# Four one-hot comparisons of 512 columns become one of 2048, and the index rows in DRAM become four times as long

## The reference

```python
x = x + attention(x, cond)                   # 16 heads, modulated by cond
x = x + sample(x, grid=cond)                 # linear interpolation along the channels
x = x + gru(cond, x)                         # 64 steps
x = x + oscillators_rk4(cond, cond, x)       # 64 steps
```

```python
ix = (grid + 1.0) * 0.5 * (L - 1)            # L = 512, clipped to the row
i0 = floor(ix)
out = (1 - w1) * x[..., i0] + w1 * x[..., i0 + 1]
```

## Time and profile before

| what | value |
| --- | --- |
| median of the runs | 1525.3 us (1524.68 to 1526.01) |
| profiled execution | 1528.0 us, span of its instructions 1526.2 us |
| TensorE busy | 1472.8 us, 97% of the span |
| VectorE busy | 1322.9 us, 87% |
| ScalarE, GpSimd busy | 902.6 us (59%), 756.9 us (50%) |
| L776, the builds | 256 instructions, 145.9 us busy |
| DMA, slices 2 to 16 of 40 | busy tenths 2 to 7, 52 to 130 GB/s |
| load of an index row | 64 of 128 KB, 3.0 us from issue to landing |
| store of an output row (L1976) | 63 of 128 KB, 1.7 us |

### The profile page before, as it was taken

One profiled execution on the slowest core, in us unless ns is written; L12 is line 12 of the kernel. 1 busy time (PEld: TensorE's weight loads), 2 busy tenths in 40 slices (PEclk: granted clock), 3 DMA queues, 4 the chain that ended last, 5 costly groups with the idle time before them and its releaser, 6 DMA issues.

```text
span 1526.2 us, 95000 instructions
## 1 busy us (share of the span) xinstructions
PE 1472.8 (97%) x42214; PEld 1308.4 (86%) x42214; DVE 1322.9 (87%) x3190; ACT 902.6 (59%) x2753; POOL 756.9 (50%) x916
## 2 busy tenths in 40 slices
PE   4799999999999999999999999999999999999997
PEld 2466677666776668999999999999999999999996
DVE  5888989988889878688888888888888888888887
ACT  5566776667766653555555555555555555555553
POOL 2567666666666754534434443443444344344432
PEclk9999999999999999999999999999999999999999
DMA  7255444545455432000000000000000000000000
GB/s 255 52 114 115 108 106 104 116 118 120 127 118 130 96 102 87 8 15 12 15 15 15 12 16 15 12 15 15 15 12 15 15 12 15 15 15 12 15 15 14
DMA packets 122602, 84.03 MB, mean 55 GB/s; under 512 B 68656, under 2 KB 107824, under 8 KB 122192
## 3 DMA queue, kind: packets, MB, share of 16 engines
q1 hardware_dynamic: 121968, 77.87, 20.3%
q10 hardware_dynamic: 224, 0.09, 0.0%
HBM read 42.23 MB, written 11.60 MB: 35 GB/s over the span
## 4 chain that ended last, share of the span: by engine, by line
PE 91%; DVE 4%; issue 2%; POOL 1%; ACT 1%; DMA 1%; SPq 0%; DVEq 0%; ACTq 0%; POOLq 0%
PE psB L1432 34%; PE psA L1461 15%; PE psQ L1146 15%; PE psA L1466 8%; PE psQ L1188 7%; PE psO L1234 5%; PE psO L1222 2%; PE psB L1170 2%; PE psA L1124 2%; DMA front<-in_cond 1%; POOL S L434 0%; DVE psO L1645 0%; POOL front L453 0%; DVE room L880 0%; PE psQ L1202 0%
## 5 line engine op out<-in xcount | busy, mean ns | idle before, releaser
L1432 PE MATMUL psB<-first,Wx 128*128 128x64 f16 x9216 | 290.3, 193 | 1.4 <-issue 1.1
L1432 PE MATMUL psB<-first,Whh 128*128 128x64 f16 x9072 | 287.0, 193 | 1.3 <-POOL first L1897 0.5
L1461 PE MATMUL psA<-ts,Cp 128*128 128x64 f16 x8160 | 280.7, 193 | 6.0 <-ACT ts L1532 6.0
L1432 PEld LDWEIGHTS psB<-first,Wx 128*128 128x128 f16 x9216 | 277.9, 98 | 2.0 <-issue 1.7
L1432 PEld LDWEIGHTS psB<-first,Whh 128*128 128x128 f16 x9072 | 274.1, 98 | 2.3 <-issue 1.4
L1146 PE MATMUL psQ<-Wx,front 128*128 128x512 f16 x1152 | 269.0, 384 | 4.1 <-DVE front L952 4.0
L1461 PEld LDWEIGHTS psA<-ts,Cp 128*128 128x128 f16 x8160 | 256.2, 98 | 7.0 <-ACT ts L1532 6.8
L1532 ACT ACTIVATE ts<-qst 128x256 f16<-128x256 f32 x192 | 80.1, 417 | 297.9 <-DVE qst L1645 297.9
L1146 PEld LDWEIGHTS psQ<-Wx,front 128*128 128x128 f16 x1152 | 108.9, 99 | 124.5 <-issue 5.0
L1897 POOL TENSOR_TENSOR en<-rz,dn 128x256 f32<-128x256 f32 x64 | 46.7, 730 | 259.8 <-issue 257.1
L1466 PE MATMUL psA<-ts,Cp 128*128 128x64 f16 x4080 | 161.2, 193 | 0.3 <-issue 0.3
(11 more groups left out here) (194 smaller groups left out, 2890.4 us busy)
## 6 DMA issues: line engine op xcount, KB each, us to landing
front<-in_x SPq DMA_DIRECT2D x32, 256.0 KB, 3.1
XR<-in_x_turned SPq DMA_DIRECT2D x32, 256.0 KB, 3.4
rows<-rows_dram SPq DMA_DIRECT2D x64, 128.0 KB, 3.0
out<-ob SPq DMA_DIRECT2D x63, 128.0 KB, 1.7
x<-x SPq DMA_DIRECT2D x29, 224.0 KB
Whh<-in_W_qkv SPq DMA_DIRECT2D x12, 256.0 KB, 8.4
room<-in_W_hh SPq DMA_DIRECT2D x12, 256.0 KB, 2.7
room<-in_W_ih SPq DMA_DIRECT2D x12, 256.0 KB, 3.0
```

The lines of the kernel that those rows point to most:

```text
L1432: last = mm(o, W_[:, i, c, g * PART:(g + 1) * PART], src[:, j, c, :], start=False, stop=False, skip_group_check=True)
L1461: mm(psF[:, s % 2, m, :], Cp[:, i, c, m * PART:(m + 1) * PART], ts_[:, 0, c, :], start=(c == 0 and m == 0 and i == 0), stop=False, skip_gr ...
```

## The change

`rows_dram` gets four versions of each index row: version c holds i0 - 128 c, so that each is to be compared with p alone. `lidx` shrinks to one column, `rows` grows from 512 to 2048 elements per partition, and `build` becomes one instruction over 2048 elements. It can't be split over two places of a slot any more, so it stands whole in one of them. `grid_rows` writes the four versions with four instructions in place of one cast. The kernel also asks for a smaller scratch area for descriptors (`dynamic_dma_scratch_size=2048`), which makes room for the longer rows.

```diff
-    lidx, gqk = sb("lidx", [PART, KC]), sb("gqk", [PART, 1])
+    lidx, gqk = sb("lidx", [PART, 1]), sb("gqk", [PART, 1])
-    rows = [sb(f"rows{u}", [PART, D], F16) for u in range(2)]
+    rows = [sb(f"rows{u}", [PART, KC, D], F16) for u in range(2)]
...
         def load_rows(p, b):
             need(sp, e_built, p.n * 2 + b - 1)
-            sp.dma_start(rows[b][:, :], rows_dram[bass.ds(p.n * 2 + b, 1), :].rearrange("a n -> (a n)")
-                         .partition_broadcast(PART)).then_inc(rows_in[b], 16)
+            sp.dma_start(rows[b][:, :, :].rearrange("p c n -> p (c n)"), rows_dram[bass.ds(p.n * 2 + b, 1), :, :]
+                         .rearrange("a c n -> (a c n)").partition_broadcast(PART)).then_inc(rows_in[b], 16)
...
-        def build(p, b, chunks):
-            if chunks[0] == 0:
-                dve.wait_ge(rows_in[b], p.n * 16 + 16)
...
-            for k in chunks:
-                e = v.tensor_scalar(E_of(p, b)[:, k, :], rows[b][:, :], lidx[:, k:k + 1], None, ALU.is_equal)
-            if chunks[-1] == KC - 1:
-                e.then_inc(e_built, 1)
+        def build(p, b):
+            dve.wait_ge(rows_in[b], p.n * 16 + 16)
...
+            v.tensor_scalar(E_of(p, b).rearrange("p c n -> p (c n)"), rows[b][:, :, :].rearrange("p c n -> p (c n)"),
+                            lidx[:, 0:1], None, ALU.is_equal).then_inc(e_built, 1)
...
-            v.tensor_copy(i0h, i0).then_inc(rows_ready, 1)
+            for c in range(KC):
+                last = v.tensor_scalar(i0h[:, c, :], i0, 1.0, float(-c * PART), ALU.mult, ALU.add)
+            last.then_inc(rows_ready, 1)
```

More of the change, by code:

```diff
@@ L179, in attention_and_sampling @@
     iint = w1.bitcast(I32)
-    i0h = rows[0][0:B, :]
+    i0h = rows[0][0:B, :, :]
     psA, psB, psQ, psO = (banks[n] for n in ("psA", "psB", "psQ", "psO"))
@@ L340, in slot @@
                 sp.wait_ge(rows_ready, 1)
-                sp.dma_start(rows_dram, i0h).then_inc(rows_out, 16)
+                sp.dma_start(rows_dram.rearrange("b c n -> b (c n)"), i0h.rearrange("b c n -> b (c n)")).then_inc(rows_out, 16)
                 sp.wait_ge(rows_out, 16)
@@ L387, in _ @@
                                 pattern=[[-1, PART]], channel_multiplier=1).then_inc(consts, 1)
-        nc.gpsimd.iota(lidx[:, :], pattern=[[PART, KC]], base=0, channel_multiplier=1,
+        nc.gpsimd.iota(lidx[:, :], pattern=[[0, 1]], base=0, channel_multiplier=1,
                        allow_small_or_imprecise_dtypes=True).then_inc(consts, 1)
@@ L761, in scale_x @@
                             rsT.unsqueeze(1).broadcast_to([PART, KC, PART]), ALU.mult).then_inc(xr_done, 1)
-        def build(p, b, chunks):
-            if chunks[0] == 0:
-                dve.wait_ge(rows_in[b], p.n * 16 + 16)
[L766 to L774, removed]
-            for k in chunks:
-                e = v.tensor_scalar(E_of(p, b)[:, k, :], rows[b][:, :], lidx[:, k:k + 1], None, ALU.is_equal)
-            if chunks[-1] == KC - 1:
-                e.then_inc(e_built, 1)
+        def build(p, b):
+            dve.wait_ge(rows_in[b], p.n * 16 + 16)
+            if p.n < NP - 1:
+                need(dve, samp_done, p.n * 2 + b - 1)
+            elif b == 1:
+                for u in range(2):
+                    dve.wait_ge(wih_out[u], 3 * KC // 2 * 16)
+            if p.n == 0:
+                dve.wait_ge(consts, 3)
+                dve.wait_ge(cp_lo, KC)
+                dve.wait_ge(wo_lo, KC)
+            v.tensor_scalar(E_of(p, b).rearrange("p c n -> p (c n)"), rows[b][:, :, :].rearrange("p c n -> p (c n)"),
+                            lidx[:, 0:1], None, ALU.is_equal).then_inc(e_built, 1)
         def means(cols, qk, x):
@@ L976, in slot @@
                 grid_middle()
-            if tap and tap.n > 0:
-                build(tap, 0, (0,))
             if p := pair(-1):
@@ L982, in slot @@
             if tap:
-                build(tap, 0, (1, 2, 3) if tap.n > 0 else range(KC))
+                build(tap, 0)
             if i == 1:
@@ L1002, in slot @@
                 grid_weight()
-            if tap:
-                build(tap, 1, (0, 1))
             if p := pair(-2):
@@ L1013, in slot @@
             if tap:
-                build(tap, 1, (2, 3))
+                build(tap, 1)
             if p := pair(-1):
@@ L1060, in _ @@
             slot(*pairs_at(i))
-        build(N3, 0, (0,))
         low_qk(N1, 0)
         low_qk(N1, 1)
-        build(N3, 0, (1, 2, 3))
+        build(N3, 0)
         sums_qk(N0, 0)
         least(N1)
-        build(N3, 1, (0, 1, 2))
         sums_qk(N0, 1)
@@ L1072, in _ @@
         scale_qk(N0)
-        build(N3, 1, (3,))
+        build(N3, 1)
         low_o(N2)
@@ L1092, in _ @@
         weigh_taps(N3, 1)
-        build(N2, 0, range(KC))
+        build(N2, 0)
         low_p(N0, 0)
         low_p(N0, 1)
-        build(N2, 1, (0,))
+        build(N2, 1)
         residual(N1)
-        build(N2, 1, (1, 2, 3))
         weigh_taps(N2, 0)
         low_o(N0)
-        build(N1, 0, range(KC))
+        build(N1, 0)
         weigh_taps(N2, 1)
-        build(N1, 1, range(KC))
+        build(N1, 1)
         residual(N0)
         weigh_taps(N1, 0)
-        build(N0, 0, range(KC))
+        build(N0, 0)
         weigh_taps(N1, 1)
-        build(N0, 1, range(KC))
+        build(N0, 1)
         dve.wait_ge(S_["th_done"], 1)
@@ L1986 @@
     from concourse.bass_utils import run_bass_kernel_spmd
-    nc = bacc.Bacc("TRN2", target_bir_lowering=False, num_devices=1)
+    nc = bacc.Bacc("TRN2", target_bir_lowering=False, num_devices=1, dynamic_dma_scratch_size=2048)
     x, cond = inputs["x"], inputs["cond_2048"]
@@ L2007 @@
     out = nc.dram_tensor("out", (T, PART, KC * B), F32, kind="ExternalOutput").ap()
-    rows = nc.dram_tensor("rows_dram", (B, D), F16, kind="Internal").ap()
+    rows = nc.dram_tensor("rows_dram", (B, KC, D), F16, kind="Internal").ap()
     wih = nc.dram_tensor("wih_dram", (D, 2, 3 * D), F16, kind="Internal").ap()
```

## The result

The changed kernel took 1528.45 us in the median of 20 executions, against 1526.67 us of the kernel before in 20 on the same chip. The two medians differ by 1.8 us; the ratio worked out from all the executions is 1.0022, with a 95% interval from 1.0012 to 1.0032: slower by some 3.4 us. Timed once more on another chip, it was 1.0033 [1.0021, 1.0045], and the kernel before against itself 0.9996 [0.9985, 1.0006]. The mean of the two ratios of the change is 1.0027, or 4.2 us of 1526. The median lies within the predicted range, and the ratio just past the 0.2% that the prediction took as no change, on the slower side. (In the excerpt of the order of the changed kernel's steady slot, the query/key subtractions stand with L748 and L751; in the profile they are L751 and L754.)

A forecast was written before the change was run, and what follows sets the result against it. TensorE, busy for 97% of the span, was taken to bound the kernel. The terms +3.0 - 0.3 + 0 + 0 gave +2.7 us, and against the median of 1525.3 a forecast of 1528.0 us, range 1524.8 to 1532.

The forecast's parts named there:

- The build: VectorE's one-hot build: one takes 0.7 to 1.8 us where four cost 1.2 to 3.0; booked at 0 in steady slots.
- The piece ahead of the subtraction: Slot at 95 us: removing a build piece before the query/key subtraction ends TensorE's 0.34 us wait, -0.3 us once.
- The index rows: Start, slot 2: four operations replace one cast on VectorE, taking turns with GpSimd; +3.0 us, handed on whole to TensorE.
- the upper: Upper bound for the index rows at the start: all three added copies take a full turn with GpSimd, +3.5 us.
- The wait for oT: Start of the kernel: the delayed copies lengthen TensorE's wait for oT from 1.18 to 4.2 us.
- The clock: TensorE's 1.2 GHz stretch, 78.36 to 81.70 us: taken as 0, with -1.7 and +1.5 us kept open.
- the rival that the loss vanishes: TensorE's low-clock loss at the start disappears, -1.7 us, giving 1526.3 us; chance 2.5 in 10.
- The loads: Row loads growing from 128 to 512 KB land at 3 to 3.5 us and cost 0 us in the slots.
- the slow rival: Row loads keep 85 GB/s, delaying x1 in the slots and the end: 1530 to 1558 us; chance 1.5 in 10.
- The tail: After the last slot: +0.2 us on the projection behind low_o(N2), -0.2 at the last build; together 0, from -0.2 to +0.5.
- the relief of TensorE: Steady slots: VectorE's saved 0.3 us reaches TensorE 26 times, worth 7.8 us, giving 1520.5; chance 0.4 in 10.
- the copies that slip through: Start: the added index copies run at their lone pace of 0.42 us each; +0.1 us, 1525.4; chance 1 in 10.

The follow-up runs named there:

- the copies alone: The kernel before with three more index-copy operations behind its cast, into spare buffers, nothing else of the change; ratio 1.0016, repeated 1.0011.
- the two with the loads twice: The changed kernel with every row load issued again into a spare buffer, 1.0094; the same with single loads in the last three pairs, 1.0055.
- the kernel with the loads alone: The kernel before with 512 KB row loads, its one cast row stored four times, comparisons reading the first quarter; ratio 1.0010, repeated 1.0022.

## Why the prediction was right, step by step

The forecast was 1528.0 and the median 1528.45, inside the range. But two terms were wrong, in opposite directions, and their errors nearly cancel: that the number came out so close is luck. It is luck, too, that 1528.45 is so near to 1528.0; the kernel before took 1526.67 in the same series, not the 1525.3 that the forecast started from. The mechanism of the copies is there, but smaller than forecast; that of the loads' cost the prediction doesn't have.

**The build, 0.7 to 1.8 us, no gain in the steady slots: right.** 0.70 to 1.46, median 0.74. The cover was TensorE's own work: VectorE's time for the builds went from 145.9 to 57.6 us, and in the same stretch its idle time grew (ahead of the sums of squares, L795, 48.8 us in 100 to 560, for ScalarE; 17.5 before). Putting the four comparisons back changed nothing either. A slot without a pause stayed at 17.25 us.

**The piece ahead of the subtraction, -0.3 us: the wait right, the gain not seen.** The wait of 0.34 at 96.63 is gone at 95.53, but the scores come 18.18 us after the last ones, where the kernel before has 18.19 with the wait.

**The index rows, +3.0 us: too large; they cost 1.40.** The turn by turn reading was right, and so was the consequence that the delay is never made up. Three of the four copies took 1.26 to 1.37 us. The step that failed is the working for where each copy gets its turn. I carried GpSimd's old row on as it stood and let the third and fourth wait for a product each; in fact VectorE got a turn between any two of GpSimd's operations, and the fourth copy needed no turn:

```profile
57.85 3.74 POOL L412 TENSOR_TENSOR Wo<-room,Wo 128x512 f16<-128x512 f32 x3
61.55 1.22 POOL L453 TENSOR_TENSOR front<-front,modA 128x512 f32<-128x512 f32 x1
62.86 1.44 POOL L453 TENSOR_TENSOR front<-front,modB 128x512 f32<-128x512 f32 x1
64.26 1.60 POOL L412 TENSOR_TENSOR Wo<-room,Wo 128x512 f16<-128x512 f32 x1
```

That is GpSimd's timeline in the changed kernel, where its operations take 1.2 to 1.6 us. In the terms of the sum: four copies take 4.07 us where one cast took 1.27, +2.8 instead of +4.3; low_cp(3) 0.93 instead of 1.30, -0.37 as forecast with -0.45; the idle 0.82 taken up as forecast. 2.8 - 0.37 - 0.82 = 1.6, of which 1.40 reach the scores. The lower bound, +0.4, supposed all three alone and was 1.0 too low; the upper, +3.5, was 2.1 too high. The exclusion of whole instructions, by the Trainium skill's "SBUF — State Buffer", section "SBUF: two separate sides", agrees with 1.26 to 1.37 for the three that took turns with GpSimd and 0.41 for the one that didn't; it gave the price of a turn, not how many would be needed.

**The wait for oT, 4.2 us: it was 1.66.** A consequence of the same step, and of the clock: with a low stretch from 59 to 63 us the projection ahead of it takes 4.29 us in this profile and eats into the wait. Without one, in the copies alone, the wait is 2.52. The place of the waiting projection moves by the 1.40 us of the copies, from 9.62 to 11.02 us after the scores. The scores at 79.7 came at 77.35, with 0.81 of the difference from the earlier start.

**The clock, 0 with both signs open: right to be open.** In the changed kernel's profile the projection at 78.77 takes 2.76 us, not 4.45, but there are low stretches elsewhere. Windows with TensorE's granted clock as the third last number:

```profile
19.00:28.00 9.00, 4.34 (x11) 1.62 (x12) 8.70 (x21) 6.92 (x16) 0.58 (x1) 0.65 0.92 312
36.00:42.00 6.00, 3.99 (x15) 2.39 (x16) 5.86 (x11) 2.00 (x5) 3.49 (x7) 0.72 0.33 89
57.00:63.00 6.00, 4.66 (x106) 2.34 (x107) 5.97 (x7) 3.16 (x7) 5.92 (x6) 0.72 0.94 123
1512.00:1517.00 5.00, 4.88 (x115) 4.89 (x116) 3.93 (x11) 1.98 (x7) 1.43 (x3) 0.66 0.10 31
```

They move in the kernel before, too: 23 to 31 and 78 to 82 us in one profile, 20 to 27, 37 to 41 and 58 to 61 in the other. This is no property of the change, and the rival that the loss vanishes can't be told from chance in one profile.

**The loads, 0 us in the slots: too small.** The rate was right against the slow rival: loads land after 4.5 us in the median where 85 GB/s alone would have needed 6.2 for the bytes, and in the changed kernel x1 is never waited for. PT is, once, 0.20 us at 81.73, one of the signs that the prediction named for being wrong; the copies alone show that wait too (0.29). By the prediction's own estimate the cover of x1 shrank from 1.9 us to 0.4: the last piece is issued at 312.03, takes 0.66 and with the 1.7 us of a store would be there at 314.4, and the samples start at 314.75 (timelines of SP and PE). The landing marks say less: 1.6 us before, 0.9 now in this slot, and over the 27 slots from 100 to 560 us 1.5 and 1.6 in the median, 1.0 and 0.5 at the least. In these slots the cover held.

```profile
312.03 0.66 SPq L302 DMA_DIRECT2D x<-x  x1
...
314.75 3.74 PE L1180 MATMUL psQ<-x,room 128*128 128x128 f16 x64
```

The step left out two things. One is that TensorE depends on the DMA engines without a semaphore, through its own instructions. The other is the first samples at 88 us, where x1 had no cover to spare in the kernels with larger loads. In the 26 slots, the mean is 449.8 us over the five kernels with 128 KB loads (449.07 to 450.71), 450.8 over the six with 512 KB (449.93 to 452.07) and 451.8 over the two with the loads twice: +1.0 and +2.0. The two groups overlap in single profiles. From there to the second row of L1262 (602.37; L1270 at 602.57 before), four of the five with small loads and four of the six with large ones have no low clock, and take 38.0 (37.7 to 38.3) and 38.5 us (38.1 to 38.9): +0.5. Together +1.5, and with the 0.7 to 1.0 us at the start in the kernel with the loads alone 2.2 to 2.5; its two timed runs say 2.4, with intervals of about 2 us to each side.

**The tail, 0: right.** 0.17 us appear at oT, and the 0.17 ahead of the last samples are gone (timeline of PE):

```profile
572.89 2.85 PE L1226 MATMUL psO<-oT,Wo 128*128 128x128 f16 x48 [0.17 <-DVE oT L862]
...
606.10 2.96 PE L1194 MATMUL psQ<-qn,room 128*128 128x64 f16 x96
```

**The rivals.** Slow loads, the relief of TensorE and the copies that slip through didn't happen. (The terms given for the first add up to 1533 to 1559, not 1530 to 1558.)

**The sum.** Copies 1.4, the slot at 95 between -0.3 and 0, the tail 0, loads 1.5 by the profiles to 2.4 by the times: 2.6 to 3.8 us. Measured 3.4 and 5.0. The experiments' ratios add up to 2.1 + 2.4 = 4.5. Each number is uncertain by one or two microseconds; that both terms are there is shown (the copies by the distance of 1.40 in every pair of kernels, the loads by the two timings of them alone taken together and by the doubling), their exact share is not. No version that I ran beats the kernel before.

## What to carry to other kernels

Relieving an engine that isn't the one that the others wait for pays nothing, even with 88 us; price the setup work of such a trade where it stands, at the start or the end where nothing has slack. Between two engines that exclude each other, price a row of operations by turns, one in each gap, and count anew how the partner's row shifts. And look at the "issue" pauses of the busiest engine before adding bytes: with more traffic that nobody waits for, the pauses between blocks of instructions grew here, in the mean of several profiles.

## What was not expected of the hardware

- TensorE's instructions arrive in packets of 16.4 KB, 256 instructions by the count, through the same DMA engines as the data. Right after transfers at 281 to 468 GB/s, TensorE once stood still for 3.0 us until such a packet was in.
- A row load that 128 partitions share runs at 85 GB/s with a row of 1 KB, and much faster with one of 4 KB: four times the bytes take 1.5 us longer to land in the median (4.5 against 3.0), and in the seven microseconds from 606 us with doubled loads the engines move up to 468 GB/s.
- One float16 comparison of 2048 elements takes 0.70 us at the least, where four of 512 take 4 x 0.30 = 1.20.
- TensorE's stretches of 1.2 GHz, 3.4 us or twice that, move from one profile to the next of one kernel; each is worth up to 1.7 us (4.45 against 2.76 for a projection), half of what this change was measured at.
